# A depthwise convolution stage: one outer tap moved from TensorE to VectorE, and a small product laid out in four column groups

## The reference, cut to what matters

```python
xz = x @ Win                                   # 128 -> 512 channels
xb, z = jnp.split(xz, 2, axis=-1)              # 256 and 256
xb = conv_general_dilated(xb, conv_w, (1, 1), ((1, 1), (1, 1)), feature_group_count=256)   # 3 x 3, one filter per channel
xb = silu(xb + conv_b)                         # called u below
x_dbl = einsum('bcl,cd->bdl', xs_flat, Wxproj) # 256 -> 10 values of a pixel: 8 for dt, B, C
...
du = delta * u ; x = exp(delta * A) * x + du * B ; y = x * C      # the scan, in four directions
```

## Time and profile before

| | us |
|---|---|
| median of 3 runs | 4086.34 |
| lowest, highest run | 4076.75, 4086.82 |
| span of the profiled execution | 4082.8 |
| its own time beside the span | not given by the page; its span alone is shown |
| the stage `convolve` in the profile (PE's first to last matmul) | 2900.2 to 3372.6 |

### The profile page before, as it was taken

The page is one execution under the profiler, slowest core; times in us unless marked ns, Lnnn a source line. Parts: engine busy times, 40 slices in busy tenths (PEclk is TensorE's granted clock), DMA queues, the critical chain, the costliest instruction groups (busy, mean ns, idle before and its releaser), DMA issues. The chain is left out here.

```text
span 4082.8 us, 72330 instructions
## 1 busy us (share of the span) xinstructions
PE 3799.2 (93%) x24506; PEld 2972.9 (73%) x24506; DVE 3212.4 (79%) x7763; ACT 2727.4 (67%) x6143; POOL 1444.1 (35%) x1715
## 2 busy tenths in 40 slices
PE   7999996999999999999999999988899995888898
PEld 5777774999889898899988898976566652333347
DVE  6899995777777777877777777769566778998885
ACT  5788884677776677766777666758544437777753
POOL 5888882000020000200001000015124467888873
PEclk8999997999999999999999999999899995777789
DMA  8877751000010000100001000022233335556557
GB/s 212 209 197 200 202 155 32 17 23 20 17 48 19 23 23 14 50 19 23 23 14 50 9 16 9 9 71 88 92 108 133 133 148 189 177 183 211 172 191 223
DMA packets 286601, 382.87 MB, mean 94 GB/s; under 512 B 41754, under 2 KB 156442, under 8 KB 285466
## 3 DMA queue, kind: packets, MB, share of 16 engines
q1 hardware_dynamic: 255466, 310.59, 24.5%
q0 software_dynamic: 29184, 67.27, 6.2%
q10 hardware_dynamic: 1584, 0.40, 0.1%
HBM read 205.45 MB, written 119.54 MB: 80 GB/s over the span
## 5 line engine op out<-in xcount | busy, mean ns | idle before, releaser
L959 ACT ACTIVATE l_ph<-l_T 128x512 fp32r<-128x512 f32 x1024 | 611.7, 597 | 550.6 <-PE l_T L864 550.6
L1076 DVE TENSOR_TENSOR l_pl<-l_T,l_ph 128x512 fp32r<-128x512 f32 x1024 | 707.1, 691 | 274.5 <-ACT l_ph L959 273.7
L1065 DVE CUSTOM_DVE_ANT_0 l_pr<-l_S,l_zero 128x512 f32<-128x512 f32 x1024 | 704.6, 689 | 76.9 <-PE l_S L787 13.5
L964 ACT ACTIVATE l_pr<-l_pr,l_st 128x512 f32<-128x512 f32 x1024 | 731.7, 715 | 1.1 <-DVE l_st L1071 1.0
L876 PE MATMUL l_O<-l_ph,l_vh 128*128 128x256 f32 x2048 | 662.0, 323 | 12.5 <-DVE l_pl L1076 12.0
L1108 POOL TENSOR_TENSOR l_xs<-l_xs,l_bob 128x128 f32<-128x128 f32 x128 | 57.1, 459 | 1646.4 <-DMA l_xs<-x 1645.3
L864 PE MATMUL l_T<-l_ident,l_pr 128*128 128x128 f32 x4096 | 613.2, 272 | 0.0
L864 PEld LDWEIGHTS l_T<-l_ident,l_pr 128*128 128x128 f32 x4096 | 508.0, 140 | 136.4 <-issue 0.2
L877 PE MATMUL l_O<-l_ph,l_vl 128*128 128x256 f32 x2048 | 578.2, 282 | 0.0
L878 PE MATMUL l_O<-l_pl,l_vh 128*128 128x256 f32 x2048 | 577.1, 282 | 0.0
L785 PE MATMUL l_S<-l_kh,l_qh 128*128 128x512 f32 x1024 | 417.3, 408 | 1.8 <-DVE l_st L1065 1.5
(11 more groups left out here) (266 smaller groups left out, 8249.6 us busy)
## 6 DMA issues: line engine op xcount, KB each, us to landing
l3b_u<-ub SPq DMA_DIRECT2D x256, 256.0 KB, 3.0
l_kq<-l_hl SPq DMA_DIRECT2D x192, 128.0 KB, 5.5
l_kq<-l_hl POOLq DMA_DIRECT2D x192, 128.0 KB, 4.2
zs<-l_tmp SPq DMA_DIRECT2D x64, 256.0 KB, 2.2
ub<-l3a_u SPq DMA_DIRECT2D x32, 512.0 KB, 3.3
l3b_z<-zs SPq DMA_DIRECT2D x64, 256.0 KB, 3.5
yz<-l3b_z SPq DMA_DIRECT2D x64, 256.0 KB, 3.3
l3b_dt<-yz SPq DMA_DIRECT2D x32, 512.0 KB, 4.4
```

Source lines behind the costliest of these rows:

```text
L959: e.activation(ph[:, i, :], psT[:, i, :], ACT.Copy).then_inc(p_hi, 1)
L964: e.activation(pr[:, s, es], pr[:, s, es], ACT.Exp, bias=st[:, s, 9:10], scale=SC, accum_out=st[:, s, 10 + k:11 + k]).then_inc(exped, 1)
L1065: e.tensor_tensor_reduce(pr[:, s, ks], psS[:, bk, :], zero[:].broadcast_to([128, 512]), 1.0, -3.0e38, ALU.add, ALU.max, st[:, s, kc:kc + 1 ...
L1076: e.tensor_tensor(pl[:, i, :], psT[:, i, :], f32(ph[:, i, :]), ALU.subtract).then_inc(p_lo, 1)
```

## The change

- The tap above the centre (row -1, column 0) leaves `outer`: 5 taps instead of 6, 15 matmuls a half instead of 18. `taps` gets a fourth scalar_tensor_tensor that reads rows 0 to 7 of `xb`, which is now 9 rows high: row 0 is the last row of the step above, and ACT copies it there for the next step (`topped`, two instructions of 64 elements, reading `xb` itself or a zero row).
- ACT's `load` comes after the copies into the planes.
- `small` becomes 8 matmuls of 128 columns, 32 output columns each (`wx` padded from 28 to 32), for four quarters q of the pixels, quarter q in column group q of the array (`tile_position=(0, 32 * q)`), so `psD` holds 128 partitions by 128. The split is two DVE instructions on 128 x 128: a copy to fp32r, and `dh * mask + psD`.
- `spread` becomes 4 matmuls of 128 columns with 128 rows and a selecting weight `selb` for each quarter. The store into `D` becomes four DMAs of 28 partitions by 128.
- On DVE `scale(g-2)` moves ahead of `taps(g, 0)`. The semaphore `D_free` goes; `small` waits for `d_done`.
- In `layer2` four more DMAs bring the weights (17 instead of 13), the preparation of `tmp`, `th`, `tl` is on 5 taps instead of 6, and POOL makes one more copy of 128 x 512 (`selb`).

The diff, cut to `convolve` (changed lines only) and the new constants:

```diff
...
     def __init__(self, nc, ctx):
-        self.th, self.tl = tile("th", [128, 6, 256], F32R), tile("tl", [128, 6, 256], F32R)
+        self.th, self.tl = tile("th", [128, 5, 256], F32R), tile("tl", [128, 5, 256], F32R)
-        self.xb = tile("xb", [128, 4, 8, 66])
-        self.ct = tile("ct", [128, 2, 3])
+        self.xb = tile("xb", [128, 4, 9, 66])
+        self.ct = tile("ct", [128, 2, 4])
-        self.wx = tile("wx", [128, 2, 28])
+        self.wx = tile("wx", [128, 2, 32])
-        self.mk = tile("mk", [28, 2])
+        self.mk = tile("mk", [128, 1])
+        self.selb = tile("selb", [128, 4, 128], F32R)
 def turned(t, d):
...
-        dh, dm = P.sb("dh", [28, 512], F32R), P.sb("dm", [28, 2, 512], F32R)
-        dl = P.sb("dl", [28, 512])
+        dh, dm = P.sb("dh", [128, 128], F32R), P.sb("dm", [128, 2, 128], F32R)
...
-        padded_hi, activated, turned_u = (P.sem(n) for n in ("padded_hi", "activated", "turned_u"))
-        padded, tapped, parts, D_free, d_done, times_B = (P.sem(n) for n in ("padded", "tapped", "parts", "D_free", "d_done", "times_B"))
+        padded_hi, activated, turned_u, topped = (P.sem(n) for n in ("padded_hi", "activated", "turned_u", "topped"))
+        padded, tapped, parts, d_done, times_B = (P.sem(n) for n in ("padded", "tapped", "parts", "d_done", "times_B"))
...
-                    e.dma_start(f32(D[32 * bb:32 * bb + 28, 512 * c0:512 * c0 + 512]), f32(dm[:, (g - 1) % 2, :])).then_inc(d_out[(g - 1) % 2], 16)
+                    for q in range(4):
+                        e.dma_start(f32(D[32 * bb:32 * bb + 28, 512 * c0 + 128 * q:512 * c0 + 128 * q + 128]), f32(dm[32 * q:32 * q + 28, (g - 1) % 2, :])).then_inc(d_out[(g - 1) % 2], 16)
...
-                w.wait_ge(d_out[s], 16 * N // 2)
+                w.wait_ge(d_out[s], 64 * N // 2)
...
-                for j in range(6):
-                    rr, cc = slice(8 * ch + 2 * (j // 3), 8 * ch + 2 * (j // 3) + 8), slice(j % 3, j % 3 + 64)
+                for j, (dr, dc) in enumerate(((0, 0), (0, 2), (2, 0), (2, 1), (2, 2))):
+                    rr, cc = slice(8 * ch + dr, 8 * ch + dr + 8), slice(dc, dc + 64)
             def small(g):
-                    w.wait_ge(D_free, g - 1)
-                products(psD[0:28, g % 2, :], [(wx[:, h, :], u_of(g, h)) for h in range(2)]).then_inc(D_full, 1)
+                    w.wait_ge(d_done, g - 1)
+                for h in range(2):
+                    for q in range(4):
+                        t = e.matmul(psD[32 * q:32 * q + 32, g % 2, 0:128], wx[:, h, :], u_of(g, h)[:, 128 * q:128 * q + 128], start=(h == 0), stop=(h == 1), tile_position=(0, 32 * q))
+                t.then_inc(D_full, 1)
             def spread(g):
-                e.matmul(psB[:], sel[0:28, 0, :], dm[:, g % 2, :], start=True, stop=True).then_inc(B_full, 1)
+                for q in range(4):
+                    t = e.matmul(psB[:, 128 * q:128 * q + 128], V.selb[:, q, :], dm[:, g % 2, :], start=True, stop=True)
+                t.then_inc(B_full, 1)
...
-                            w.wait_ge(tapped, 4 * (g - 2) + 2 * h + 2)
-                        e.activation(xb[:, (2 * g + h) % 4, :, 1:65], ps[:, i, :].rearrange("p (r c) -> p r c", c=64), ACT.Copy).then_inc(free[i], 1)
+                            w.wait_ge(tapped, 6 * (g - 2) + 3 * h + 3)
+                        e.activation(xb[:, (2 * g + h) % 4, 1:9, 1:65], ps[:, i, :].rearrange("p (r c) -> p r c", c=64), ACT.Copy).then_inc(free[i], 1)
...
-                        w.wait_ge(tapped, 4 * (g - 1) + 2 * h + 2)
+                        w.wait_ge(tapped, 6 * (g - 1) + 3 * h + 3)
-                if g < N:
-                    for m in loads(g):
-                        load(m)
+                if g + 1 < N:
+                    for h in range(2):
+                        bi, bt = bank(f"b{h}", g)
+                        w.wait_ge(free[bi], bt + 1)
+                        if g:
+                            w.wait_ge(tapped, 6 * (g - 1) + 3 * h + 3)
+                        above = xb[:, (2 * g + h) % 4, 8, 1:65] if g % 8 < 7 else f32(xh[:, 0, 1:65])
+                        e.activation(xb[:, (2 * g + 2 + h) % 4, 0, 1:65], above, ACT.Copy).then_inc(topped, 1)
...
+                if g < N:
+                    for m in loads(g):
+                        load(m)
         def vector(e):
...
-                V = xb[:, (2 * g + h) % 4]
+                X = xb[:, (2 * g + h) % 4]
-                e.scalar_tensor_tensor(u, V[:, :, 0:64], ct[:, h, 0:1], ps[:, i, :].rearrange("p (r c) -> p r c", c=64), ALU.mult, ALU.add).then_inc(free[i], 1)
+                e.scalar_tensor_tensor(u, X[:, 1:9, 0:64], ct[:, h, 0:1], ps[:, i, :].rearrange("p (r c) -> p r c", c=64), ALU.mult, ALU.add).then_inc(free[i], 1)
-                e.scalar_tensor_tensor(u, V[:, :, 1:65], ct[:, h, 1:2], u, ALU.mult, ALU.add).then_inc(tapped, 1)
-                w.wait_ge(tapped, 4 * g + 2 * h + 1)
-                e.scalar_tensor_tensor(u, V[:, :, 2:66], ct[:, h, 2:3], u, ALU.mult, ALU.add).then_inc(tapped, 1)
+                e.scalar_tensor_tensor(u, X[:, 1:9, 1:65], ct[:, h, 1:2], u, ALU.mult, ALU.add).then_inc(tapped, 1)
+                w.wait_ge(tapped, 6 * g + 3 * h + 1)
+                e.scalar_tensor_tensor(u, X[:, 1:9, 2:66], ct[:, h, 2:3], u, ALU.mult, ALU.add).then_inc(tapped, 1)
+                w.wait_ge(tapped, 6 * g + 3 * h + 2)
+                if g:
+                    w.wait_ge(topped, 2 * (g - 1) + h + 1)
+                e.scalar_tensor_tensor(u, X[:, 0:8, 1:65], ct[:, h, 3:4], u, ALU.mult, ALU.add).then_inc(tapped, 1)
             def small(g):
-                e.tensor_copy(dh[:], psD[0:28, j, :]).then_inc(parts, 1)
-                w.wait_ge(parts, 2 * g + 1)
-                e.tensor_tensor(dl[:], psD[0:28, j, :], f32(dh[:]), ALU.subtract).then_inc(D_free, 1)
-                w.wait_ge(D_free, g + 1)
-                e.tensor_scalar(dl[:], dl[:], mk[:, 0:1], None, ALU.mult).then_inc(parts, 1)
-                w.wait_ge(parts, 2 * g + 2)
+                e.tensor_copy(dh[:], psD[:, j, 0:128]).then_inc(parts, 1)
+                w.wait_ge(parts, g + 1)
-                    w.wait_ge(d_out[j], 16 * (g // 2))
+                    w.wait_ge(d_out[j], 64 * (g // 2))
-                e.scalar_tensor_tensor(dm[:, j, :], f32(dh[:]), mk[:, 1:2], dl[:], ALU.mult, ALU.add).then_inc(d_done, 1)
+                e.scalar_tensor_tensor(dm[:, j, :], f32(dh[:]), mk[:, 0:1], psD[:, j, 0:128], ALU.mult, ALU.add).then_inc(d_done, 1)
             def scale(g):
...
+                if g >= 2:
+                    scale(g - 2)
-                if g >= 2:
-                    scale(g - 2)
...
+    selb = np.zeros((4, 32, 4, 128), np.float32)
+        selb[q, 24:26, q] = 1.0
+    o["selb"] = selb.reshape(128, 4, 128)
+    low[:, 4] = -np.tile(low[0:32, 0], 4)
```

More of the change, by code:

```diff
@@ L1120, in layer2 @@
         win = K.planes[:, 1, 1, 0:512]
-        raw, t1, t2, selr = (K.acc[:, 0, a:b] for a, b in ((0, 1024), (1024, 2048), (2048, 3072), (3072, 3328)))
+        raw, t1, t2, selr, selbr = (K.acc[:, 0, a:b] for a, b in ((0, 1024), (1024, 2048), (2048, 3072), (3072, 3328), (3328, 3840)))
         cA, cD, cm = K.cc[:, 0:8], K.cc[:, 8:16], K.cc[:, 16:18]
@@ L1173, in sync, with spread_tap @@
                 fetch(b)
-            for dst, src in ((win, io["L3_conv_Win"]), (V.tmp[:, 0:3, :], io["taps"][0:3].rearrange("(a t) c -> a t c", a=1).broadcast_to([128, 3, 256])),
-                             (V.tmp[:, 3:6, :], io["taps"][6:9].rearrange("(a t) c -> a t c", a=1).broadcast_to([128, 3, 256])),
-                             (V.ct[:, 0, :], io["taps"][3:6, 0:128].rearrange("t p -> p t")), (V.ct[:, 1, :], io["taps"][3:6, 128:256].rearrange("t p -> p t")),
-                             (V.wx[:], io["wx28"].rearrange("(h p) d -> p h d", p=128)), (V.cb[:], io["L3_conv_conv_b"].rearrange("(h p) -> p h", p=128)),
-                             (V.mk[:], io["low"][0:28, 0:2]), (cA, io["L3_conv_A_log"].rearrange("(k p) a -> p (k a)", p=128)),
+            def spread_tap(k):
+                return io["taps"][k:k + 1].rearrange("(a t) c -> a t c", a=1).broadcast_to([128, 1, 256])
+            for dst, src in ((win, io["L3_conv_Win"]), (V.tmp[:, 0:1, :], spread_tap(0)), (V.tmp[:, 1:2, :], spread_tap(2)),
+                             (V.tmp[:, 2:5, :], io["taps"][6:9].rearrange("(a t) c -> a t c", a=1).broadcast_to([128, 3, 256])),
+                             (V.ct[:, 0, 0:3], io["taps"][3:6, 0:128].rearrange("t p -> p t")), (V.ct[:, 1, 0:3], io["taps"][3:6, 128:256].rearrange("t p -> p t")),
+                             (V.ct[:, 0, 3:4], io["taps"][1:2, 0:128].rearrange("t p -> p t")), (V.ct[:, 1, 3:4], io["taps"][1:2, 128:256].rearrange("t p -> p t")),
+                             (V.wx[:], io["wx32"].rearrange("(h p) d -> p h d", p=128)), (V.cb[:], io["L3_conv_conv_b"].rearrange("(h p) -> p h", p=128)),
```

(23 more changed lines are left out.)

3 lines of the change are left out of this document (2 added, 1 removed).

## The result

| | before | after |
|---|---|---|
| median of 4 runs, us | 4081.55 | 4013.23 |
| lowest, highest | 4069.41, 4086.82 | 4004.65, 4020.02 |
| span of the profiled execution | 4082.8 | 4017.8 |

The ratio is 0.983 [0.9807, 0.9853]: 68 us faster on the medians, 65 on the profiles, where 80 were forecast. The time lies in the range given, 7 us above the predicted one, and the sign was right. Of the 12 us of gain that are missing, 5 don't show in the time: the forecast subtracted from a median before of 4086.3, and with a fourth run it is 4081.55. That much of the hit is luck. (The profiled execution after took 4020.02 us, 2.2 more than its span.)

What follows compares the result with a forecast made beforehand. PE was taken as the bound; gains of 19.9 us in image 0, 39.5 in images 1 and 2, 19.8 in image 3 and 1 in the tail made 80, so 4086.3 became 4006 us, range 3990 to 4043.

Steps and rivals of the forecast that it cites:

- What bounds it: Whole stage: PE is the bound, needing 11.45 us a step after the change, from 14.17.
- The tap: PE's outer product: one tap fewer removes 6 matmuls x 0.237 = 1.42 us a step, all on the path.
- small in column groups: PE's small product: 16 passes at 0.033 us plus 0.2 for the ends, 0.73 for 2.03, saving 1.30.
- the drain that the Trainium skill names: PE at small's tiling mode changes: a drain of 0.2 us at most, read from the attention product.
- spread: PE's spread as four matmuls of 128 columns: between -0.2 and +0.2 us a step, taken as 0.
- DVE's taps and small: DVE's step: 8.9 us undisturbed; first tap at most 749 ns, others to some 1750; small's two instructions 0.65 with gaps.
- ACT's two copies: ACT: two copies of 64 elements, at most 0.75 us each, hidden at 7.3 of 11.5 us.
- SP's queue: Loop from taps to taps over u's store: 10.8 to 11.5 us; 0.25 a step set aside in images 1 and 2.
- image 3: Last image's eight steps: 14.68 us to 12.2 each, with POOL and two more stores queued, 19.8 us gained.
- (a): Rival at taps from step 8: DVE with POOL and the queue become the bound, saving 49 us, 4037; chance 0.17.
- (b): Rival at small: column groups run one after another, small stays 1.99 us, saving 47, 4039; chance 0.07.
- (c): Rival at SP's queue: dm issues from 1.44 us lengthen the loop; at 1.8, 41 us slower, 4127; chance 0.04.

Runs made afterwards that it cites:

- e3: The changed kernel with small, its split, spread and dm's one store as before; tap moved, ACT and DVE orders new: 4035.99 us, 0.9889 of the kernel before.
- e4: The changed kernel without the tap: six outer taps on PE, small in column groups, ACT and DVE orders new: 4035.14 us, 0.9888 of the kernel before.
- e5: The changed kernel with only u's store moved ahead of dm's stores, the planes' store left behind them: 3997.22 us, 0.9784 of the kernel before.
- e9: The changed kernel with u's and the planes' stores ahead of dm's, plus a second outer tap moved to DVE: 4000.32 us, 0.9798 of the kernel before.
- e6: The changed kernel with dm stored in eight DMAs of 28 x 64 instead of four: 4090.31 us, 1.0018 of the kernel before.

## Why the prediction was right, and where it was off

**What bounds it.** Right: PE's own work, in 22 of the 30 steps from 1 to 30 (11.18 to 11.25 us from step 2 on; step 1 is 10.76 long and has no spread). The halves show it one by one (12.66 and 12.70 for 14.13).

**The tap, 1.42 us a step.** Right: e3 gives 14.13 - 12.66 = 1.47, and e4 1.43 for all of the other half.

**small in column groups, 0.73.** It measured 0.78, saved 1.25 for 1.30. The attention product of the first layer was the right row: 0.033 us a pass there, 0.036 here. On the drain that the Trainium skill names (TensorEngine Tiling (Array Packing), section Key Properties): what both changes of mode cost outside the passes is in 0.78 - 0.58 = 0.20 us, as estimated. A drain that hides inside the 0.58 is not excluded; it would make the passes cheaper than 0.036.

**spread, 0.** It measured 0.17 cheaper, inside the bounds of 0.2; the low end was the nearer one. A PE step came to 11.24 for 11.45.

**DVE's taps and small.** Right: the first tap never over 751 ns, the others up to 2206 (the forecast had some 1750), small's two 281 and 348 ns (0.65 with gaps). The new tap (L1711) means 1049 ns, and DVE still fits.

**ACT's two copies.** They take 0.25 us each, for a bound of 0.75.

**SP's queue.** Half right. The 4.9 us for taps and small in its loop stood without a working; from taps(g, 0) to the issue of dm's stores the trace has 4.6 in image 1 (from 3040.55) and 5.9 in image 3 (from 3278.69), with POOL beside the taps. I had its loop at 10.8 to 11.5 us and put 0.25 us on each of 16 steps and more on image 3. In images 1 and 2 the 14 steps away from the planes' stores pay nothing (11.24), and image 3 pays more than forecast: its 7 steps came to 88.61, 12.66 each, for 12.2. 5.1 us of that are step 28, 4.9 the loop with POOL. Its base was read too high as well: the forecast took 14.68 for each step of image 3 before, but the first three are 14.07 to 14.13, and the seven make 100.93 in place of 102.8.

**The term that was missing** is the planes' store, on which the sum is silent. I costed dm's four issues and u's store and asked of each queue what it was moved past, but not what the biggest transfer in it does to a shorter step; "Moving its load behind the planes lets the xb copies start about 2 us sooner" counted what the load gains and not how long all of ACT's queue stands when it is late. The sign was in the trace of before. ACT as a timeline, step 20 of the kernel before:

```profile
3186.72 0.64 ACT L1629 ACTIVATE l_xh<-ahead 128x512 fp32r<-128x512 f32 x1 [10.49 <-DMA ahead<-x3t]
```

An idle time of 10.49 us that cost 0.4 (the step was 14.55), as long as a step was 14.13 and ACT had room. At 11.24 the same wait costs 5.4 and 6.6 us in steps 12 and 20, and in step 28 the wait for z's store, with what the loop adds, 5.1. This term of three steps, 17 us, is the largest between the 80 forecast and the 65 that came. e5 shows that it is not the planes' store alone: u's store in the wrong place makes 10 of these 17. Against the 17 stand 0.46 us in each of 16 steps (7 us; 0.21 of it PE's own, 0.25 what I had set aside for the queue) and 1 us of image 0. The rest of image 3 comes out even: 0.96 a step set aside, 6.7 us, against 4.9 of the loop and 1.8 of the base. The start of the stage and step 0, which vary from run to run, add 6 to the loss.

**The rivals.** (a) did not come with this change but with the next tap (e9). (b) fell by the 0.58 us of 16 passes, where one after another they would have taken 1.8. (c) fell as priced, an issue being 0.752 us (longest 1.802) for the 1.44 that it needed; e6, which doubles the issues, brings its loop about and takes the whole gain.

## What to carry to other kernels

When the bound engine's step gets shorter, look again at every wait of the profile before that cost nothing, the big rare transfer first: what 14.1 us a step hid, 11.2 did not. In a DMA queue that one engine issues in order, put what closes the tightest loop (here the store that frees a buffer) first, and a large store where the queue has its longest pause. One block of six lines moved up was worth 25 us on top of the 68 of the change, and nothing without it.
